# Attention layers of eight heads on one core: small products cut into 32-column pieces, and replica copies issued two at a time

## The reference

```
h = group_norm(x) * gamma + beta
q, k, v = wq @ h + bq, wk @ h + bk, wv @ h + bv     # (B, 128, 1024)
# blocks 1 and 2: split into 8 heads of 16 channels; blocks 3 and 4: one head
w = softmax(scale * q^T k, axis=-1)                 # 1024 x 1024 for each head
x = x + wo @ (v w^T) + bo
```

## Time and profile before

| | |
|---|---|
| median of the runs | 2206.46 us (2204.09, 2206.46, 2207.37) |
| the profiled execution, its own time | 2202.45 us |
| its span in the trace | 2200.7 us |
| granted TensorE clock over the span | 0.997 of 2.4 GHz |
| busy: TensorE, VectorE, ScalarE, GpSimd | 96%, 82%, 78%, 24% |
| eight-head blocks, steady stretch | about 80 us to about 1620 us |

### The profile page before, as it was taken

How to read it: one execution, slowest core, us unless ns; L and a number is a source line. 1 busy time by engine, 2 the same in 40 slices (tenths; PEclk the granted TensorE clock), 3 DMA queues, 4 the chain that set the end, 5 groups by cost and what they waited for, 6 DMA issues and landing times. The chain is left out here.

```text
span 2200.7 us, 59773 instructions
## 1 busy us (share of the span) xinstructions
PE 2103.0 (96%) x24652; PEld 1090.8 (50%) x24652; DVE 1810.8 (82%) x3176; ACT 1713.7 (78%) x3107; POOL 521.2 (24%) x689
## 2 busy tenths in 40 slices
PE   2999999999999999999999999999979999999998
PEld 0244444434344443444444344444438888888887
DVE  2888889888898988889898988989837777777776
ACT  1378787787878778787777878777778888888887
POOL 3113030312303031230303123030023333333331
PEclk9999999999999999999999999999999999999999
DMA  6053334526243351633335263443111111112111
GB/s 75 13 80 54 64 60 64 80 56 92 49 69 61 61 80 52 96 53 65 63 67 83 49 90 53 65 64 64 35 55 49 56 60 44 64 39 69 46 44 51
DMA packets 81747, 133.95 MB, mean 61 GB/s; under 512 B 17632, under 2 KB 50528, under 8 KB 81504
## 3 DMA queue, kind: packets, MB, share of 16 engines
q1 hardware_dynamic: 78240, 129.70, 32.8%
q10 hardware_dynamic: 3264, 0.79, 0.2%
HBM read 53.12 MB, written 17.83 MB: 32 GB/s over the span
## 5 line engine op out<-in xcount | busy, mean ns | idle before, releaser
L449 DVE TENSOR_REDUCE h_half_nmax<-h_s_ps 128x1 f32<-128x512 f32 x2048 | 1281.8, 684 | 176.8 <-PE h_s_ps L683 155.5
L600 ACT ACTIVATE h_probs<-h_st_ps 128x512 f32<-128x512 f32 x2048 | 1099.9, 601 | 306.1 <-PE h_st_ps L683 293.6
L683 PE MATMUL h_s_ps<-h_krep,h_qrep 96*32 96x512 bf16 x8192 | 822.7, 386 | 44.1 <-SPq L234 29.2
L683 PE MATMUL h_st_ps<-h_qrep,h_krep 99*32 99x512 bf16 x8192 | 810.5, 381 | 15.0 <-ACT h_probs L600 10.7
L674 PE MATMUL h_pv<-h_probs,h_vT 128*32 128x512 f32 x4096 | 534.9, 594 | 2.5 <-issue 1.5
L683 PEld LDWEIGHTS h_s_ps<-h_krep,h_qrep 96*32 96x32 bf16 x8192 | 227.5, 96 | 441.1 <-DVE h_half_nmax L449 211.1
L683 PEld LDWEIGHTS h_st_ps<-h_qrep,h_krep 99*32 99x32 bf16 x8192 | 229.4, 97 | 344.0 <-ACT h_probs L600 152.5
L1339 PE MATMUL o_s<-o_k,o_q 128*128 128x512 f32 x768 | 224.4, 428 | 8.1 <-DVE o_q L1160 5.8
L349 POOL TENSOR_SCALAR h_nparts<-h_nmax 128x16 bf16<-128x16 f32 x64 | 16.3, 255 | 896.4 <-DVE h_nmax L457 896.4
L1339 PE MATMUL o_pv<-o_pT,o_vT 128*128 128x512 f32 x768 | 208.1, 406 | 0.8 <-ACTq L1266 0.8
L1154 DVE TENSOR_TENSOR o_pT<-o_t,o_pT 128x512 fp32r<-128x512 f32 x256 | 164.5, 684 | 44.1 <-ACT o_pT L1291 41.6
(11 more groups left out here) (116 smaller groups left out, 1316.7 us busy)
## 6 DMA issues: line engine op xcount, KB each, us to landing
h_krep<-h_kp SPq DMA_DIRECT2D x96, 256.0 KB, 8.9
h_qrep<-h_qp SPq DMA_DIRECT2D x192, 128.0 KB, 6.5
x_res<-out_dram SPq DMA_DIRECT2D x24, 512.0 KB, 3.8
num<-av SPq DMA_DIRECT2D x128, 64.0 KB
rrep<-rden_dram SPq DMA_DIRECT2D x16, 512.0 KB
out_dram<-o_y SPq DMA_DIRECT2D x16, 512.0 KB
out_dram<-h_y SPq DMA_DIRECT2D x15, 512.0 KB, 2.6
o_x_in<-out_dram SPq DMA_DIRECT2D x15, 512.0 KB, 3.5
```

Source lines behind the costliest of these rows:

```text
L449: reduce = nc.vector.tensor_reduce(half_nmax[:, c, unit:unit + 1], s_ps[bank(2 * n + c)][:, :], AX.X, ALU.max, negate=True)
L600: nc.scalar.activation(probs[g % 2][:, j, :], st_ps[bank(n)][:, :], ACT.Exp, scale=1.0 / CH ** 0.5).then_inc(exp_done, 1)
L683: product = nc.tensor.matmul(to[columns, :], stationary[:, columns], moving, start=True, stop=True)
```

## The change

It has two parts. In the shared bank, averages, values and maximum rows become products of 32 columns as well: one average becomes 4 matmuls, one values job 16 in place of 4, and a transpose becomes 2 matmuls by the identity, of 32 and 16 columns, with a float32 result in place of bfloat16. On SyncE, from the second image on, each copy of a stack term waits until the copy two before it has landed (two semaphores, used in turn; a term of q is two DMAs), and the wait for the maximum rows stands in the middle of q's six terms, no longer ahead of them.

```diff
@@ replicate
+                def await_turn(n):
+                    if rows is not None and n >= 2:
+                        sp.wait_ge(rep_dma[n % 2], landing[n % 2])
+
+                def copy(n, to, source):
+                    sp.dma_start(to, source).then_inc(rep_dma[n % 2], 16)
+                    landing[n % 2] += 16
+
                 sp.wait_ge(parts_ready, 2 * u + 1)
                 for term, part in enumerate((0, 1, 2, 0, 1, 0)):
-                    sp.dma_start(krep[par][term * CH:(term + 1) * CH, :, :], parts["k"][:, part, :]).then_inc(rep_dma, 16)
+                    await_turn(term)
+                    copy(term, krep[par][term * CH:(term + 1) * CH, :, :], parts["k"][:, part, :])
                 sp.wait_ge(parts_ready, 2 * u + 2)
-                if rows is not None:
-                    sp.wait_ge(mrow_dma, 16 * rows)
                 for term, part in enumerate((0, 0, 0, 1, 1, 2)):
+                    if term == 3 and rows is not None:
+                        sp.wait_ge(mrow_dma, 16 * rows)
+                    await_turn(TERMS + term)
                     for th in range(2):
-                        sp.dma_start(qrep[par][term * CH:(term + 1) * CH, th, :, :],
-                                     parts["q"][:, part, th * HALF:(th + 1) * HALF]).then_inc(rep_dma, 16)
-                sp.wait_ge(rep_dma, 16 * 3 * TERMS)
-                sp.sem_inc(rep_dma, -16 * 3 * TERMS)
+                        copy(TERMS + term, qrep[par][term * CH:(term + 1) * CH, th, :, :],
+                             parts["q"][:, part, th * HALF:(th + 1) * HALF])
+                for n in range(2):
+                    sp.wait_ge(rep_dma[n], landing[n])
+                    sp.sem_inc(rep_dma[n], -landing[n])
@@ project_values, average, transpose_max
-                    product = nc.tensor.matmul(misc[:, n * P:(n + 1) * P], h[:, t * P:(t + 1) * P],
-                                               weights, start=True, stop=True)
+                    product = in_columns(misc[:, n * P:(n + 1) * P], h[:, t * P:(t + 1) * P], weights)
-                nc.tensor.matmul(misc[:, 0:2], gmat[:, :], st2[:, :], start=True, stop=True).then_inc(misc_for_dve, 1)
+                in_columns(misc[:, 0:2], gmat[:, :], st2[:, :]).then_inc(misc_for_dve, 1)
-                nc.tensor.transpose(misc_bf[0:3 * MH, 0:P], nparts[th][:, :, :].rearrange("p a b -> p (a b)"),
-                                    ident[:, :]).then_inc(misc_for_act, 1)
+                rows = nparts[th][:, :, :].rearrange("p a b -> p (a b)")
+                for first in range(0, 3 * MH, 32):
+                    some = slice(first, min(first + 32, 3 * MH))
+                    product = nc.tensor.matmul(misc[some, 0:P], rows[:, some], ident[:, :], start=True, stop=True)
+                product.then_inc(misc_for_act, 1)
```

More of the change, by code:

```diff
@@ L164, in many_heads @@
         misc = psum("misc", [P, HALF])
-        misc_bf = misc[:, :].bitcast(BF16)
         consts = sem("consts")
@@ L198, in many_heads @@
         g_in = sem("g_in")
-        rep_dma, load_dma, av_dma, den_dma, store_dma = (
-            sem(n) for n in ("rep_dma", "load_dma", "av_dma", "den_dma", "store_dma"))
+        rep_dma = [sem(f"rep_dma{i}") for i in range(2)]
+        load_dma, av_dma, den_dma, store_dma = (
+            sem(n) for n in ("load_dma", "av_dma", "den_dma", "store_dma"))
         act_own, dve_own, pool_own = sem("act_own"), sem("dve_own"), sem("pool_own")
@@ L220, in replicate @@
             def replicate(par, u, rows=None):
+                landing = [0, 0]
+                def await_turn(n):
[4 more added lines that the diff above has]
+                    landing[n % 2] += 16
                 sp.wait_ge(parts_ready, 2 * u + 1)
                 for term, part in enumerate((0, 1, 2, 0, 1, 0)):
-                    sp.dma_start(krep[par][term * CH:(term + 1) * CH, :, :], parts["k"][:, part, :]).then_inc(rep_dma, 16)
+                    await_turn(term)
+                    copy(term, krep[par][term * CH:(term + 1) * CH, :, :], parts["k"][:, part, :])
                 sp.wait_ge(parts_ready, 2 * u + 2)
-                if rows is not None:
-                    sp.wait_ge(mrow_dma, 16 * rows)
                 for term, part in enumerate((0, 0, 0, 1, 1, 2)):
+                    if term == 3 and rows is not None:
+                        sp.wait_ge(mrow_dma, 16 * rows)
+                    await_turn(TERMS + term)
                     for th in range(2):
-                        sp.dma_start(qrep[par][term * CH:(term + 1) * CH, th, :, :],
-                                     parts["q"][:, part, th * HALF:(th + 1) * HALF]).then_inc(rep_dma, 16)
-                sp.wait_ge(rep_dma, 16 * 3 * TERMS)
-                sp.sem_inc(rep_dma, -16 * 3 * TERMS)
+                        copy(TERMS + term, qrep[par][term * CH:(term + 1) * CH, th, :, :],
[3 more added lines that the diff above has]
+                    sp.sem_inc(rep_dma[n], -landing[n])
                 sp.sem_inc(rep_ready, 1)
@@ L548, in max_rows @@
                 act.wait_ge(misc_for_act, n)
-                own.mark(nc.scalar.copy(mrow[th][:, :], misc_bf[0:3 * MH, 0:P]))
+                own.mark(nc.scalar.copy(mrow[th][:, :], misc[0:3 * MH, 0:P]))
             def send_max_rows(step, th):
```

## The result

| | before | changed |
|---|---|---|
| median of the runs (four each) | 2205.28 us (2202.99 to 2207.37) | 2148.76 us (2148.39 to 2149.79) |
| the profiled execution, its own time | 2202.45 us | 2148.40 us |
| its span | 2200.7 us | 2146.5 us |
| granted clock over the span | 0.997 | 0.997 |

The ratio is 0.9748, with a 95% interval of 0.9733 to 0.9764: 56.5 us faster by the medians, 54.2 us by the two spans. The forecast was 46 to 48 us less, and the time lies in its range of 2143 to 2184, but 1.2 us under the 2150 to 2168 of the forecast itself: nearest to the rival "more than I count" (2148).

What follows compares the result with a forecast made beforehand. TensorE's array, nearly full in the eight-head blocks, plus its waits, was taken as the bound. Savings of 12.2 + 9.9 + 3.8 + 17.7 + 3.8 = 47.4 us, less 1.4, gave 2158 us; range 2143 to 2184.

Steps and rivals of the forecast that it cites:

- more than I count: Rival: smaller delays of fetches and of the maximum rows in other groups vanish as well, 2148 us; chance 10%.
- Maximum rows: Shared-bank transposes on TensorE, 64 times: from 0.27 to 0.08 us each, 12.2 us saved (7 to 14).
- Values: Shared-bank values jobs on TensorE, 32 times: from 1.19 to 0.88 us each, 9.9 us saved.
- Averages: Shared-bank averages on TensorE, 16 times: from 0.41 to 0.17 us each, 3.8 us saved (0 to 5.8).
- Given back to VectorE and ScalarE: Eight-head passes: 1.4 us charged for places where VectorE or ScalarE now ends the wait.
- Stacks: TensorE's wait at group 20 for late stacks, in 15 passes, goes: 17.7 us saved.
- SyncE's account: SyncE's queue, two terms in flight: k complete about 417 us, q near 433, TensorE asks at 438.2; 5 us spare.
- Fetches: TensorE's instruction fetches behind k's burst come in time; three breaks of about 1.3 us go, 3.8 us saved.
- The new products are some 110 more TensorE instructions in a pass, 4%: Remark within the fetches term: instructions added on TensorE by the column products, given without a time.
- The rate of instructions: Rival: TensorE can't take 64 instructions in 0.86 us; values cost 1.75 us, 2196 us in all; chance 8%.
- The throttle: Rival on SyncE: each term takes 3.1 to 3.3 us, stacks come as late as now, 2176 us; chance 8%.
- The slower rival: Copies in effect one at a time, 4.5 us a term, 2400 us; decides from 3.4 us a term; chance 4%.

Runs made afterwards that it cites:

- r_short: Changed kernel with each values product cut once more, into 64 moving columns, giving twice the products: 2148.88 us (one run).
- early half alone: Kernel with old products, half of q's terms ahead of the maximum-rows wait, no limit on copies in flight: 2186.23 us, ratio 0.9926 to before.
- q_unlimited: Changed kernel without the limit of two copies in flight, half of q's terms still ahead of the maximum rows: 2198.25 us, ratio 0.9968 to before.
- p_products: Kernel before with the column products alone, SyncE's copies as before: 2211.25 us, ratio 1.0031.
- p_two: Kernel before with the limit of two terms in flight alone, old products, all of q's copies behind the maximum rows: 2225.43 us, ratio 1.0101.

## Why the prediction was right, and where it was off

The direction, and most of the size, came from terms that the runs bear out.

- *Maximum rows* (predicted 0.08 each, 12.2 us saved): about 0.05, the share by columns, some 14 us. The lower bound was the value.
- *Values* (0.88, 9.9 us): 0.88, 10.1 us.
- *Averages* (0.17, 3.8 us): 0.06 to 0.09, 5.7 us. Of the two numbers that I stood between, 0.44 and 0.05, the one without a rate was true, and r_short says why. The Trainium skill's "TensorEngine Tiling (Array Packing)", Performance Considerations, gives some 60 cycles of overhead for a matmul, from which I had estimated 0.20 us. If these 25 ns ran one after another for all matmuls, r_short's values would take 1.6 us, and they took 0.89. If each column group has them for itself, they can't be seen here, since a group has 56 ns for each of its sixteen; the average's 0.06 us, with two matmuls in each column group, would fit that. The averages have the fewest moving columns of all, and still gained 0.36 us each.
- *Given back to VectorE and ScalarE* (1.4 us): by distances the jobs save 29.8 us; by runs (2175.37 to 2148.76) 26.6, and by group lengths 25.5 in 15 of the 16 passes. By the two, some 3 us are given back.
- *Stacks* (17.7 us): 19.8 by group lengths. Of the 2.1 us between them 1.7 are the 3.4 us at half clock behind the first break: I had read the break of the earlier trace rows and not what follows it. SyncE's account held nearly in full: from the first copy of k to the signal 31.7 us predicted, 417.8 - 385.1 = 32.7 measured. Spare was to be 5 us and is 3.1. The maximum rows at group 16, beside q's third term, cost nothing.
- *Fetches* (3.8 us): 6.7 us. Here the term was undersized: by group lengths the three large stops cost 2.6, 1.5 and 1.5 us where I counted 1.3 each, and two of about 0.6 us, in passes 7 and 9, were not counted.

So the miss of 8 us is the sum of small ones: 1.8 + 1.9 + 2.1 + 2.9 us from maximum rows, averages, stacks and fetches, less 1 to 2 for what was given back. That is the rival "more than I count" in its time and partly in its reason.

One step was wrong, though the sum hid it: **"The new products are some 110 more TensorE instructions in a pass, 4%"**, with no price. I treated products and copies as two changes that add. Without the limit, the new products cost 12 us where they should gain 26.6, so the limit, priced at 3.8 us with the fetches, is worth 49.5 us beside the new products. In the traces I counted TensorE's instructions (matmuls and weight loads) between the starts of two of its fetches, each of 16 KB and usually some 250 instructions apart. The largest distances are 491 before, 498 with the early half alone and 528 with the products alone, all three with stops, and 357 in the changed kernel, 384 with three in flight and 418 in r_short, all without. Read at the stops themselves the number is closer: counted from the start of one fetch to the stop that the next one ends, 426 to 526 instructions pass at the 39 stops of over 0.6 us (the longest of each pass, in groups 11 to 13) of the five kernels that have them, 509 at the median; some records are missing, which lowers a count. So about 510 instructions, two fetches' worth, are what TensorE works off before it stands still; 96 more of them stand in groups 8 and 11, and k's copies last through the same stretch. Had the change been made without the limit, I would have forecast some 2162 us and met 2198.

*The rivals.* The rate of instructions is ruled out (r_short). The throttle doesn't eat the gain: a term takes 2.7 us over the twelve and 2.9 for q's six, not 3.1 to 3.3. The slower rival is sound in its price, and 2.7 us a term is clear of its point of decision, given as 3.4 (by its own terms, 2 us behind the 439.1 of before, it is (441.1 - 401.4) / 12 = 3.3).

**Open.** Why a fetch waits behind k's copies and much less behind q's wasn't settled. k's six are 1.57 MB in one burst, and the early q copies half of that; whether size, or number, or what else runs then decides, no run tells; q_unlimited, with its stops in group 14, shows that the fetches aren't quite free of the copies there either. The stock of instructions is read from the stops; no run varied it by itself.

## What to carry to other kernels

A TensorE at 96% busy can still lose time to its own instructions: look for stops inside a group, with "issue" as the reason, and for what the DMA queues did in the 15 us before; an edit that adds instructions there has to be priced together with the copies beside it. If every product around a small job has 32 columns, give the job 32 columns too, even at four times the instructions. Ask of a part what it is worth with and without the other parts: here the same products are worth -12 or +27 us.

## What the runs showed of the hardware

- TensorE stood still for missing instructions once about 510 of them (426 to 526 as read) had passed since the start of a fetch, and went on 3.0 to 3.8 us after the next fetch's packets began. With 96 more instructions in the stretch the stops were more and longer: five of 0.7 to 2.1 us before, twelve of 0.9 to 4.6 us in p_products.
- Behind some stops of 2 to 4.6 us, whether for instructions (5 of 12 passes of p_products) or for a semaphore (7 of 15 of p_two), the granted clock was 0.50 for 3.4 us, once 6.8: the same matmul groups are 0.43 us apart, not 0.22.
- Among groups of 32 stationary columns the same values job cost 0.24 us more in pieces of 64 columns and 0.31 more in 128; two products of 32 and 16 columns with 128 moving bfloat16 columns cost about 0.05 us.
- Two copies in flight do as well as three (2148.8 and 2148.6 us), and one costs 4.3 us for 256 KB where two give 2.7, 2.9 for q's.
- A semaphore decrement in TensorE's queue takes 0.15 us, and eleven in a row stop the array for 1.5 us.
